# Routing flags by pairs of tiles, path weights ahead of the tokens' third part, and root's output added later, in a one-core graph layer

## The reference, cut to what matters

```python
for _ in range(DEPTH + 1):                      # 8 levels, 255 nodes
    all_nodes.append(current)
    score = einsum('td,td->t', flat_x, w1s[current]) + b1s[current]
    all_logits.append(score)
    choice = ((sign(score) + 1.0) / 2.0).astype(int32)
    current = current * 2 + choice + 1
path_weights = gelu(abs(logits))
for i in range(DEPTH + 1):
    t_i = einsum('td,tdo->to', flat_x, w2s[nodes_i]) + b2s[nodes_i]
    out = out + t_i * path_weights[:, i][:, None]
```

## Time and profile before

| What | Value |
|---|---|
| median of 3 runs | 361.04 us |
| the profiled execution | 361.46 us |
| its span (first to last instruction) | 359.6 us |
| PE busy | 329.1 us, 92% |
| DVE busy | 229.0 us, 64% |
| ACT busy | 150.8 us, 42% |
| POOL busy | 122.0 us, 34% |
| share of PE in the chain that ended last | 87% |
| DMA moved | 79.09 MB, mean 220 GB/s |

### The profile page before, as it was taken

The page is one execution under the profiler, slowest core; times in us unless marked ns, Lnnn a source line. Parts: engine busy times, 40 slices in busy tenths (PEclk is TensorE's granted clock), DMA queues, the critical chain, the costliest instruction groups (busy, mean ns, idle before and its releaser), DMA issues.

```text
span 359.6 us, 9058 instructions
## 1 busy us (share of the span) xinstructions
PE 329.1 (92%) x2631; PEld 239.1 (66%) x2638; DVE 229.0 (64%) x653; ACT 150.8 (42%) x468; POOL 122.0 (34%) x240
## 2 busy tenths in 40 slices
PE   0999999999999999999899999999999998999920
PEld 0577869996878888767455666566666664567810
DVE  4745767946350541847989776889876666567740
ACT  2355546404042150138043665445465665444610
POOL 8000000004000000715802555565555554454555
PEclk9999999999999999989999999999999999999985
DMA  6971415619999000000526599999999999998005
GB/s 176 297 153 41 129 43 128 170 59 341 387 387 347 1 0 2 1 0 0 195 99 234 206 390 387 384 386 385 387 362 389 386 385 386 386 387 324 6 6 66
DMA packets 52595, 79.09 MB, mean 220 GB/s; under 512 B 3447, under 2 KB 20035, under 8 KB 52548
## 3 DMA queue, kind: packets, MB, share of 16 engines
q1 hardware_dynamic: 51138, 77.09, 61.8%
q0 software_dynamic: 720, 0.64, 1.6%
q10 hardware_dynamic: 690, 0.77, 0.7%
HBM read 77.21 MB, written 1.30 MB: 218 GB/s over the span
## 4 chain that ended last, share of the span: by engine, by line
PE 87%; DVE 5%; issue 2%; POOL 2%; DMA 1%; POOLq 1%; ACT 1%; ACTq 0%; DVEq 0%
PE ps L1289 84%; PE ps L1292 3%; DVE reg L1282 1%; DMA reg<-in_x_dram 1%; POOL reg_w L596 1%; POOL out_dram L607 1%; POOLq L115 1%; DVE acc L850 1%; DVE cols L1151 0%; DVE reg L1145 0%; DVE colp L1157 0%; DVE acc L976 0%; ACTq L615 0%; DVE rank L1142 0%; DVE colp L1153 0%
## 5 line engine op out<-in xcount | busy, mean ns | idle before, releaser
L1289 PE MATMUL ps<-reg 128*64 128x256 f32 (+8 forms) x1444 | 224.7, 311 | 0.6 <-DVE reg L1145 0.2
L1289 PEld LDWEIGHTS ps<-reg 128*64 128x64 f32 (+5 forms) x1446 | 152.5, 142 | 13.1 <-issue 1.3
L1289 PE MATMUL ps<-reg,reg_w 128*64 (+1 forms) x688 | 156.8, 387 | 1.6 <-issue 1.6
L1289 PEld LDWEIGHTS ps<-reg,reg_w 128*64 128x64 f32 (+1 forms) x688 | 94.5, 140 | 51.8 <-issue 8.0
L596 POOL TENSOR_TENSOR reg_w<-reg_w 128x128 f32 x150 | 72.3, 482 | 82.9 <-ACT reg_w L821 74.6
L1237 DVE SCALAR_TENSOR_TENSOR reg_w<-reg_w,nid,reg 128x128 f32 x167 | 64.0, 387 | 33.4 <-PE ps L1289 31.2
L820 ACT COPY reg_w<-ps 64x128 f32<-64x128 f32 x150 | 39.4, 263 | 62.6 <-PE ps L1289 62.6
L1237 DVE SCALAR_TENSOR_TENSOR reg<-reg_w,reg 128x128 f32 x150 | 51.4, 343 | 0.2 <-issue 0.2
L821 ACT COPY reg_w<-ps 64x128 f32<-64x128 f32 x150 | 39.2, 261 | 3.6
L1065 DVE BATCH_NORM_STATS2 stats<-ps 128x6 f32<-128x256 f32 x15 | 6.5, 432 | 29.1 <-PE ps L1289 28.9
L1289 PE MATMUL ps<-reg_w,reg 128*128 128x256 f32 (+2 forms) x106 | 25.0, 367 | 0.0
(11 more groups left out here) (243 smaller groups left out, 283.4 us busy)
## 6 DMA issues: line engine op xcount, KB each, us to landing
reg<-in_L_ffn_w2s_dram SPq DMA_DIRECT2D x127, 512.0 KB, 11.5
reg<-in_edge_attr_dram SPq DMA_DIRECT2D x13, 336.0 KB
reg<-in_L_gnn_Wc_dram SPq DMA_DIRECT2D x3, 512.0 KB, 6.2
reg<-in_L_gnn_Wn_dram SPq DMA_DIRECT2D x3, 256.0 KB, 5.2
out_dram<-acc SPq DMA_DIRECT2D x1, 512.0 KB
reg<-in_edge_attr_dram SPq DMA_DIRECT2D x13, 39.0 KB
reg<-in_L_mix_w_qkv_dram ACTq DMA_DIRECT2D x1, 384.0 KB, 5.3
reg<-in_x_dram ACTq DMA_DIRECT2D x2, 128.0 KB, 2.8
```

What stands on the lines that cost most here:

```text
L1289: return e.matmul(to, lhsT, rhs, start=start, stop=stop, skip_group_check=True)
```

## The change

The flags are made in three steps, by what lies in one PSUM bank: tiles 0 and 1, tiles 2 and 3, tile 4. ACT's absolute values and Gelu move ahead of the casts of the second part. On POOL, onpath moves ahead of the third part, and the additions of root's output (with the clearing of acc2 behind them) wait for colp_ready instead of for the last Pm. On PE, p_root is raised by root's last product, and the 8 zero matmuls and the one that raised p_root are gone. The sorting of half 0 is split: first parts 0 and 1 of all tiles, then, after x_rest 4, part 2 of all tiles.

```diff
--- before.py
+++ after.py
@@ -568,13 +568,13 @@
                 e.wait_ge(x_cut, q + 1)
                 e.tensor_tensor(rest[:, parts, :], xf[:, parts, :], xp[:, 0, parts, :], ALU.subtract).then_inc(x_rest, 1)
             e.wait_ge(path_ready, 1)
+            e.wait_ge(s_gw, 1)
+            e.tensor_tensor(onpath[:, :, 0:NODES], gw[:, :, 0:NODES], path[:, :, 1:NODES + 1], ALU.mult).then_inc(g_gw, 1)
             for q, parts in enumerate((slice(0, NT - 1), slice(NT - 1, NT))):
                 e.wait_ge(x_cut, q + 3)
                 e.wait_ge(x_rest, q + 1)
                 e.tensor_tensor(xp[:, 2, parts, :], rest[:, parts, :], xp[:, 1, parts, :], ALU.subtract).then_inc(x_rest, 1)
-            e.wait_ge(s_gw, 1)
-            e.tensor_tensor(onpath[:, :, 0:NODES], gw[:, :, 0:NODES], path[:, :, 1:NODES + 1], ALU.mult).then_inc(g_gw, 1)
-            e.wait_ge(v_Pm, NT)
+            e.wait_ge(colp_ready, 1)
             for i in range(NT):
                 e.wait_ge(s_root, i + 1)
                 e.tensor_tensor(acc[:, i, :], acc[:, i, :], root[:, i, :], ALU.add).then_inc(g_acc, 1)
@@ -773,16 +773,17 @@
             c(e.activation(shares[:, 0:1], ones[:, 0:1], ACT.Gelu))
             e.wait_ge(xn_ready, 2 * NT)
             cut(0, 1, xf)
+            e.wait_ge(v_side, 2)
+            c(e.activation(gw[:, 0:4, 0:NODES].rearrange("p (b t) n -> p b t n", b=2), lg_pairs, ACT.Abs))
+            e.wait_ge(v_side, 3)
+            e.activation(gw[:, 4, 0:NODES], ps[:, 7, 0:NODES], ACT.Abs).then_inc(s_abs, 1)
+            c.wait()
+            e.wait_ge(s_abs, 1)
+            e.activation(gw[:, :, 0:NODES], gw[:, :, 0:NODES], ACT.Gelu).then_inc(s_gw, 1)
             e.wait_ge(x_rest, 1)
             cut(1, 0, rest)
             e.wait_ge(x_rest, 2)
             cut(1, 1, rest)
-            e.wait_ge(v_side, 2)
-            c(e.activation(gw[:, 0:4, 0:NODES].rearrange("p (b t) n -> p b t n", b=2), lg_pairs, ACT.Abs))
-            e.activation(gw[:, 4, 0:NODES], ps[:, 7, 0:NODES], ACT.Abs).then_inc(s_abs, 1)
-            c.wait()
-            e.wait_ge(s_abs, 1)
-            e.activation(gw[:, :, 0:NODES], gw[:, :, 0:NODES], ACT.Gelu).then_inc(s_gw, 1)
             e.wait_ge(s_gw, 1)
             e.wait_ge(p_root, 1)
             for i in range(NT):
@@ -1110,13 +1111,13 @@
             norm_end(NT - 1, NT)
 
 
-            for to, frm, n in ((side[:, 0:4, 0:NODES, :].rearrange("p (b t) n s -> p b t n s", b=2), lg_pairs, NT - 1),
-                               (side[:, 4, 0:NODES, :], ps[:, 7, 0:NODES], NT)):
-                e.wait_ge(p_lg, n)
-                c(e.tensor_scalar(to[..., 0], frm, 0.0, None, ALU.is_le))
-                e.tensor_scalar(to[..., 1], frm, 0.0, None, ALU.is_gt).then_inc(v_side, 1)
+            for i, n in ((0, 2), (2, 2), (4, 1)):
+                e.wait_ge(p_lg, i + n)
+                frm = ps[:, LG_AT[i][0], 0:n * NODES].rearrange("p (t n) -> p t n", t=n)
+                c(e.tensor_scalar(side[:, i:i + n, 0:NODES, 0], frm, 0.0, None, ALU.is_le))
+                e.tensor_scalar(side[:, i:i + n, 0:NODES, 1], frm, 0.0, None, ALU.is_gt).then_inc(v_side, 1)
             c(e.memset(path[:, :, 1:2], 1.0))
-            e.wait_ge(v_side, 2)
+            e.wait_ge(v_side, 3)
             c.wait()
             for l in range(LEVELS - 1):
                 n = 2 ** l
@@ -1579,9 +1580,8 @@
             logits(4)
             for i in range(NT):
                 for k in range(2):
-                    mm(ps[:, i, D:2 * D], hT[:, k, i * TP:(i + 1) * TP], w_root[:, k, :], k == 0, k == 1)
-            keep_busy(4, 8)
-            mm(ps[:, 4, 0:D], zeros_b[:, 0:128], zeros_b[:, 0:D], False, False).then_inc(p_root, 1)
+                    ins = mm(ps[:, i, D:2 * D], hT[:, k, i * TP:(i + 1) * TP], w_root[:, k, :], k == 0, k == 1)
+            ins.then_inc(p_root, 1)
 
 
 
@@ -1609,20 +1609,22 @@
                ).then_inc(p_pre, 1)
 
 
-            def sort_tokens(k, i):
+            def sort_tokens(k, i, parts):
                 e.wait_ge(v_Pm, i + 1)
-                for q in range(3):
+                for q in parts:
                     for n, (c0, c1) in enumerate(HALF):
                         ins = mm(ps[:, 2 * k + n, 0:c1 - c0], xp[:, q, i, k::2], Pm[:, i, c0:c1],
                                  q == 0 and i == 0, q == 2 and i == NT - 1)
-                if i == NT - 1:
+                if q == 2 and i == NT - 1:
                     ins.then_inc(p_sort, 2)
             e.wait_ge(s_root, NT)
             keep_busy(3, 8)
+            for i in range(NT):
+                sort_tokens(0, i, range(2))
             e.wait_ge(x_rest, 4)
             for i in range(NT):
-                sort_tokens(0, i)
-            sort_tokens(1, 0)
+                sort_tokens(0, i, range(2, 3))
+            sort_tokens(1, 0, range(3))
             e.wait_ge(colp_ready, 1)
             for i in range(NT):
                 for n, (c0, c1) in enumerate(HALF):
@@ -1640,7 +1642,7 @@
                 mm(ps[:, (4, 7)[n] if t < 0 else 5 + n if t == 0 else 7, 0:c1 - c0], sel[:, ORDER[t] if t >= 0 else 0, :],
                    leaf_rows[:, c0:c1], True, True).then_inc(p_spread, 1)
             for i in range(1, NT):
-                sort_tokens(1, i)
+                sort_tokens(1, i, range(3))
                 if i == 2:
                     e.wait_ge(s_rows, 1)
                     e.wait_ge(pool_tabs, 1)
```

## The result

The changed kernel takes 361.88 us, the median of 20 executions (360.71 to 366.21), the kernel before 360.59 (358.94 to 362.65, 20 executions). The ratio is 1.005, with a 95% interval from 1.0026 to 1.0073: some 0.5% slower. It is worked out from all fast executions of both kernels, which is why it isn't quite the ratio of the two medians (1.0036). The profiled execution took 363.25 us, 1.4 us more than the median; its span is 361.5 us.

What follows compares the result with a forecast made beforehand. The loop's start, set by the later of PE's queue and DVE's last table before "steps", was taken to bound the kernel: 2 us won, given back in table stalls, so 361.04 + 0.1 = 361.1 us, range 358.8 to 362.7.

Steps and rivals of the forecast that it cites:

- no change: Whole kernel: about 0.3% (1.1 us) is what a measurement can tell from it; chance of same 0.40.
- rival 1: DVE's tables beside POOL go through, PE decides: 1.97 us earlier, 359.1 us; 36%.
- rival 2: DVE's tables starve beside POOL, PE idles, its clock may fall: together 362.6 us; decides above 2.8 us stall; 18%.
- Flags, zeros, line 1134, ranks: Routing before Pm: counts 1.62 us earlier, line 1134 held by onpath, line 1139 and Pm only 0.87 earlier.
- colp: DVE's four 40-element instructions, without POOL: 2.75 to 0.96 us; colp_ready at 177.2, PE's queue 1.97 us earlier.
- The tables beside POOL: DVE's tables during POOL's sums and clearing: 2.8 us stall, last table at 184.64, 0.1 us later, deciding.
- The gap and the clock: PE idle ahead of "steps", 182.7 to 185.6, granted clock falling: 0.7 to 1.7 us more; only in rival 2.
- The test that the prediction set: Last table instruction: 184.6 by the forecast, 182 by rival 1, 185.5 with clock under 1 by rival 2.
- rival 3: Fewer zeros on PE after 167 us and a 0.9 us gap before sorting drop the clock: 361.9 us; 4%.
- The loop moves with its start: PE's main loop: its end and its pauses around 301 us shift by whatever its start shifts.
- The slower rival: Same as rival 2: one 0.15 us table instruction let through per POOL instruction, stall 3.7 us, last table 0.9 later.

Runs made afterwards that it cites:

- b2: The kernel before with only p_root moved to root's last product and the 9 zero matmuls behind it removed: 360.25 us, ratio 0.9987.
- b3: The kernel before with only the flags by pairs (and ACT's wait for the third pair): 362.73 us, ratio 1.0064.
- a3: The changed kernel with 9 zero matmuls on PE ahead of its wait for DVE's tables: 361.23 us, ratio 1.0008 to the kernel before.
- a1: The changed kernel with POOL's root sums and clearing put back to wait for the last Pm: 359.29 us, ratio 0.9964 to the kernel before.
- a2: The changed kernel with root's output not added at all and acc2 cleared once Pm is complete: 358.24 us, ratio 0.9925 to the kernel before.
- b4: The kernel before with flags by pairs and the zero matmuls removed, all else in the old order: 359.29 us, ratio 0.9965.
- c2: c1 with onpath in two instructions around DVE's leaf-number instruction, third part of tiles 3 and 4 after Pm, two early sums, three in the loop: 356.98 us.
- b5: b3 with onpath on POOL made to wait for v_cnt, raised just ahead of DVE's line 1134: 360.64 us, ratio 0.9999 to the kernel before.
- c1: The changed kernel with ACT clearing acc2, POOL adding root's tiles 0 to 2 after Pm and tiles 3 and 4 in the loop: 358.06 us.
- b1: The kernel before with only root's sums and the clearing made to wait for colp_ready: 363.92 us, ratio 1.0101.

## Why the prediction was right or wrong

The forecast was 361.1 us, 0.1 more than before; it came out as 361.88, 1.3 us above the kernel that ran beside it, which is past the bound of 1.1 us that the prediction set for "no change". The time lies in the stated range, but that says little: the range, 358.8 to 362.7, takes in rival 1 and rival 2 as well, and the profiled execution, 363.25, lies above it. What the rows do bear out is the mechanism, 2 us won ahead of the sums and given back by DVE's tables beside them; what the forecast didn't have is the clock behind it. Counted from the first score product:

- **Flags, zeros, line 1134, ranks.** Forecast 0.87 earlier for line 1139, with line 1134 released by onpath: measured 13.38 against 14.22, 0.84 earlier. Right, for the reason given; b2 shows the same exclusion taking all that PE had gained, b3 more than DVE had.
- **colp.** Forecast 2.75 shrinks to 0.96, colp_ready 2.67 earlier, PE's colp products 1.97 earlier: measured 0.95 (176.58 to 177.53), 2.65 and 2.01 (20.59 against 22.60). Right. (The 4.97 us of sorting in that sum isn't the 5.05 of rows 2; from the first sorting matmul to the first colp product it measured 4.99.)
- **The tables beside POOL.** This term was sized too low. Forecast: stall of 2.8 us, last table 0.07 later than before. Measured: from 177.47, where the tables start, to 185.40 it is 7.93 us instead of 4.75, a stall of 3.2; last table 0.53 later. DVE did go on between POOL's instructions, two or three small ones each time. The clearing cost it up to 0.85 (the reduction at 181.11 took 1.12 instead of 0.27), about the 0.88 that I had set; that leaves some 0.47 of each addition's 0.68 us, not 0.38.
- **The gap and the clock.** The forecast left this out; it stood in rival 2, with 18%, which was to decide once the stall is above 2.8 us, as it is. The gap is 2.40 us, less than that rival's 2.9, and the clock fell in the profiled execution all the same, at a cost of 2.0 us (a3) where the rival had set 0.7 to 1.7. Beside the 0.5 of the tables this is the larger part of what the forecast missed there; the changed kernel's median, 1.3 us above the kernel before, can't hold all of both.
- **The test that the prediction set.** The last table was to come at 184.6 by the forecast, at 185.5 and with a clock under 1 by rival 2. It came at 185.40, which is 185.10 in the count of the profile before, and with a clock of 0.50 from 186 us: in time between the two, by the clock the sign of rival 2. The outcome is therefore a milder form of rival 2 rather than the forecast with a small error.
- **Rival 1** (the tables go through) is excluded by the rows, rival 3 (the zeros mattered) by a1, a2 and b4, whose clock held at 1.00 behind the removed zeros.
- **The loop moves with its start.** From the loop's first product to the end of the span it is 168.1 us before, 167.2 after, 167.4 without sums and 167.2 in c2 (354.2 - 187.0): right within a us. The pauses moved along: in slices of 2 us from 296 on, PE is first busy for less than 1.8 of 2.00 us in the slice from 302 before, from 304 after and from 298 in c2.

The Trainium skill ("SBUF — State Buffer", "Who interferes with whom") says that the order of issue decides who waits. b3 and b5 agree, with 3.03 and 0.82 us for the same instruction. It also says that the other "fully blocks"; the rows agree for each single instruction (0.67 instead of 0.15), while DVE's queue as a whole went on in the gaps between POOL's instructions. The slower rival's assumption of one per gap was too strict.

## What to carry to other kernels

Work moved off one engine's critical stretch lands beside another's: before a GpSimd instruction is moved, look at what VectorE does in the place where it goes, and put it beside reductions (1.82 us with it and without) and PSUM reads (a flag instruction of 510 elements took 0.74 us beside GpSimd, 0.73 without), not beside chains of small SBUF instructions: here one of them waited for each GpSimd instruction, 0.56 to 0.69 us instead of 0.15. Where the two exclude each other, a wait that fixes the order of issue can be worth more than an earlier start. And a wait of PE for 2 us costs more than itself if the clock falls in it: in the profile of a3, nine zero matmuls ahead of the wait kept the clock at 2.4 GHz. The largest gain, though, came from moving the sums and the clearing to where nobody met them (c1, c2).

## What the runs showed that was not expected

- An event 1.1 us earlier made the kernel 0.6% slower (b3), by changing the order of two issues that lay 0.1 us apart.
- The granted clock fell to half at a gap of 2.07 us ahead of the sorting (b3), and behind gaps of 2.3 to 2.4 us (changed kernel, b1), but not with a gap of 1.41 us (b2) or 1.09 us (a1, a2). The gap isn't all that counts: ahead of the routing, where all kernels run the same instructions, the half clock stood between 150 and 157 us in eight of the twelve profiles, between 42 and 48 us in three (the changed kernel, b2, b5), and at both places in b4.
- Reductions ran beside POOL's additions in 1.82 us (a1), the same as in the changed kernel, where POOL was idle beside them, while a cast of 40 elements next to them took 0.69 instead of 0.20.
